# Adjacency blocks turned by DMA, one gathered tile looked up, twelve low parts by GpSimd

## What is computed

```python
# layer 0: 8 nearest neighbours by ctx, 4 blocks
idx = top_k(-d2, 8)
for i in range(4):
    p = leaky_relu(points, 0.01)
    g = group(p, idx)
    points = (w_center[i] @ p + sum_k(w_neighbor[i] @ g)) / 9 + points
# layer 1: 30 nearest neighbours by the same ctx
rel = pts[idx30] - pts                       # 3 coordinates
feat = [rho, theta, phi] and the same minus their mean
h = 3 small layers with batch norm and leaky_relu(0.2)
att = softmax(h)                             # over the 30 neighbours
out = x + sum_k(att * x[idx30])
```

## Time and profile before

| | us |
|---|---|
| median of 3 runs | 698.96 |
| lowest, highest | 698.92, 703.58 |
| the profiled execution, its own time | 703.56 |
| its span | 701.8 |
| TensorE busy | 679.3 (97%) |
| VectorE busy | 599.0 (85%) |
| ScalarE busy | 346.1 (49%) |
| GpSimd busy | 394.1 (56%) |

### The profile page before, as it was taken

How to read it: one execution, slowest core, us unless ns; L and a number is a source line. 1 busy time by engine, 2 the same in 40 slices (tenths; PEclk the granted TensorE clock), 3 DMA queues, 4 the chain that set the end, 5 groups by cost and what they waited for, 6 DMA issues and landing times.

```text
span 701.8 us, 13118 instructions
## 1 busy us (share of the span) xinstructions
PE 679.3 (97%) x5364; PEld 573.4 (82%) x5364; DVE 599.0 (85%) x879; ACT 346.1 (49%) x529; POOL 394.1 (56%) x324
## 2 busy tenths in 40 slices
PE   5999999999999999999999999999999999999998
PEld 4799889878888887788888987987988877778887
DVE  4699999999789899876679998776895999788866
ACT  6456547347525327766694354384473434233210
POOL 2268757664877877310039677558669865610143
PEclk9999999999999999999999999999999999999999
DMA  9630300200000022644532721713627763621125
GB/s 350 192 4 2 120 1 2 90 21 11 1 2 0 2 65 87 221 152 165 164 114 91 116 79 63 118 61 91 105 76 221 126 90 90 182 77 47 46 92 164
DMA packets 39483, 64.89 MB, mean 92 GB/s; under 512 B 16000, under 2 KB 16256, under 8 KB 39424
## 3 DMA queue, kind: packets, MB, share of 16 engines
q1 hardware_dynamic: 30288, 44.61, 18.9%
q0 software_dynamic: 8608, 18.40, 13.7%
q10 hardware_dynamic: 528, 1.05, 0.4%
HBM read 47.92 MB, written 14.82 MB: 89 GB/s over the span
## 4 chain that ended last, share of the span: by engine, by line
PE 60%; DVE 16%; POOL 11%; issue 5%; ACT 4%; DMA 2%; another core or an unknown queue 1%; SPq 0%; POOLq 0%; DVEq 0%; ACTq 0%
PE bank L1669 17%; PE bank L1731 4%; PE bank L1579 4%; PE bank L1693 4%; PE bank L1581 4%; PE bank L1580 4%; PE bank L1694 4%; PE bank L1695 4%; POOL more L660 4%; PE bank L1834 3%; PE bank L1793 3%; PE bank L1836 3%; PE bank L1835 3%; POOL p_second L590 3%; POOL pts_l L601 2%
## 5 line engine op out<-in xcount | busy, mean ns | idle before, releaser
L1669 PE MATMUL bank<-nbr,pts_h 128*128 128x512 f32 (+2 forms) x512 | 192.9, 379 | 3.2 <-POOL pts_l L601 1.6
L1669 PE MATMUL bank<-nbr,pts_l 128*128 128x512 f32 (+2 forms) x512 | 190.1, 374 | 0.0
L590 POOL TENSOR_TENSOR p_second<-p_first,p_second 128x512 f32<-128x512 f32 x58 | 76.4, 1320 | 99.4 <-ACT p_second L868 99.3
L1669 PEld LDWEIGHTS bank<-nbr,pts_h 128*128 128x128 f32 x512 | 96.6, 189 | 20.8 <-POOL pts_l L601 3.4
L1669 PEld LDWEIGHTS bank<-nbr,pts_l 128*128 128x128 f32 x512 | 96.7, 189 | 14.9 <-issue 0.2
L882 ACT CAST pts_h<-bank 128x512 fp32r<-128x512 f32 (+2 forms) x64 | 35.1, 554 | 144.5 <-PE bank L1669 136.0
L1693 PE MATMUL bank<-wT,pts_h 128*128 128x512 f32 x256 | 102.7, 401 | 1.4 <-DVE pts_l L1172 0.7
L1695 PE MATMUL bank<-wT,pts_l 128*128 128x512 f32 x256 | 100.4, 392 | 0.0
L1694 PE MATMUL bank<-wT,pts_h 128*128 128x512 f32 x256 | 100.2, 392 | 0.0
L601 POOL TENSOR_TENSOR pts_l<-p_second,pts_h 128x512 fp32r<-128x512 f32 x58 | 79.1, 1370 | 3.5 <-ACT pts_h L874 2.0
L1579 PE MATMUL bank<-pts_h 128*128 128x512 f32 (+3 forms) x192 | 68.9, 359 | 8.6 <-DVE pts_l L1098 8.1
(11 more groups left out here) (228 smaller groups left out, 1518.5 us busy)
## 6 DMA issues: line engine op xcount, KB each, us to landing
p_rows<-p_second SPq DMA_DIRECT2D x32, 256.0 KB, 2.0
more<-a_rows SPq DMA_DIRECT2D x16, 480.0 KB, 4.7
scratch<-a_rows SPq DMA_DIRECT2D x14, 480.0 KB, 5.0
X<-in_ctx SPq DMA_DIRECT2D x12, 512.0 KB, 6.1
out_dram<-X SPq DMA_DIRECT2D x15, 256.0 KB
more<-in_ctx SPq DMA_DIRECT2D x4, 512.0 KB, 5.7
X<-in_x SPq DMA_DIRECT2D x2, 1024.0 KB, 5.5
x_rows<-X SPq DMA_DIRECT2D x8, 256.0 KB
```

Source lines behind the costliest of these rows:

```text
L590: pool.tensor_tensor(p, a, b, ALU.subtract).then_inc(s_p32, 1)
L1669: mm = pe.matmul(bank[u % 3][:, 0:w], p[:, m, t * P:(t + 1) * P], nbr[b][:, m, hf * HALF:hf * HALF + w], start=(m == 0 and part_ == 0), st ...
```

## The change

- The blocks of the adjacency are turned by 16 DMA transposes on SP's queue instead of 128 TensorE transposes, and land in SBUF: row blocks 0 to 6 in the place of nbr0's last eighth, the others in scratch. SP takes turns 0 and 1 ahead of the loads of X for batch 0, turns 2 to 5 and 6 to 9 ahead of the two loads for batch 1, the rest behind them.
- Row block 0 is looked up like the others (32 lookups instead of 30); the table in DRAM, its three stores and the 30 gathers go.
- The low parts of q of units 10 to 15 (pass 1) and 16 to 21 (pass 2) are made by GpSimd; ScalarE copies the bank to one of three buffers in scratch for it, right behind the high part.
- Tables: VectorE's selection ends at step 39 instead of 43, with 4 steps in step 0 instead of 6, and 6 in step 16 instead of 2; adjacency in steps 4, 7, 10, 14 instead of 3, 6, 9, 14; `G0` 42 instead of 44, `M0` 60 instead of 61; network entries 0 to 10 a step earlier, then an empty step; ScalarE's arctan a step after VectorE's entry 10. `T0` is step 109 in both.

```diff
+        with nc.sbuf_tensor("nbr0_land", [P, NT, N], F32) as nbr0_land:
+            pass
         nbr0 = sb("nbr0", [P, NT, N], F32R)
...
+        def landing(T):
+            if T < NT - 1:
+                c0 = (NT - 1) * P + T % 2 * P // 2
+                return nbr0_land[:].bitcast(BF16)[:, :, 2 * c0:2 * c0 + P]
+            o = (SC + 1) * N + T % 2 * HALF
+            return scratch[:, o:o + HALF].bitcast(BF16).rearrange("p (m n) -> p m n", m=NT)
...
+        Q_POOL = [2 * CT + j for j in range(2, 8)] + [4 * CT + j for j in range(6)]
+        q32 = [scratch[:, 6 * N - (3 - i) * HALF:6 * N - (2 - i) * HALF] for i in range(3)]
+
+        def pooled(u):
+            return sum(q <= u for q in Q_POOL)
...
-            n = STEPS_AT[g % 16] + {0: 4, 1: 1}.get(g, 0)
+            n = STEPS_AT[g % 16] + {0: 2, 1: 1, 15: 1, 16: 4, 18: 1, 20: 1, 22: 1, 34: 1}.get(g, 0)
...
-        ADJ_AT = {3: (8, 9), 6: (10, 11), 9: (12, 13), 14: (14, 15)}
+        ADJ_AT = {4: (8, 9), 7: (10, 11), 10: (12, 13), 14: (14, 15)}
...
-        ROWS_AT = {30: 0, 33: 1, 36: 2, 44: 3}
+        ROWS_AT = {28: 0, 31: 1, 34: 2, 41: 3}
...
-        G0 = max(SEL_AT) + 1
-        M0 = G0 + LOOKUPS // 2 + 2
+        G0 = 16 * 2 + 10
+        M0 = G0 + TILES + 2
...
-               ((8, 1),), ((9, 0),), ((9, 1),), ((9, 2),), (10,), (11,), (12,), (13,), (14,), (15,), (16,), ((21, 0),),
+               ((8, 1),), ((9, 0),), ((9, 1),), ((9, 2),), (10,), (), (11,), (12,), (13,), (14,), (15,), (16,), ((21, 0),),
...
+            def adj_turn(T):
+                sp.wait_ge(s_diag, T + 1)
+                if T == NT - 1:
+                    sp.wait_ge(s_sqmm, 2 * NH)
+                if T >= 2:
+                    sp.wait_ge(s_nbr, T - 1)
+                sp.dma_start_transpose(landing(T), adj[:, T % 2, :]).then_inc(s_adjT[T % 2], 16)
+
+            adj_turn(0)
+            adj_turn(1)
             for i, (t0, t1) in enumerate(((0, 4), (4, 8))):
...
+                for T in (range(6, 10) if i else range(2, 6)):
+                    adj_turn(T)
...
+            for T in range(NT + 2, TILES):
+                adj_turn(T)
+            sp.wait_ge(s_nbr, TILES)
...
+            def q_low(g):
+                pool.wait_ge(s_q32, pooled(g))
+                pool.tensor_tensor(q_l[:, g % (2 * CT), :], q32[pooled(g) % 3], q_h[:, g % (2 * CT), :].bitcast(F32),
+                                   ALU.subtract).then_inc(s_qlp, 1)
...
-                    for i in range(done, done + GATHER_AT.get(g, 0)):
...
-                        pool.indirect_dma_start(
-                            out=near_rows[:, i // K1, i % K1, :], out_offset=None, in_=tab_d,
...
+                    if s_ < 2 * CT and 2 * CT * it + s_ in Q_POOL:
+                        q_low(2 * CT * it + s_)
...
             def nbr_out(T):
-                act.wait_ge(s_adjT, T + 1)
+                act.wait_ge(s_adjT[T % 2], 16 * (T // 2 + 1))
...
-                         bank[6 + T % 2][:].bitcast(BF16).rearrange("p (m n) -> p m n", m=NT)) \
-                    .then_inc(s_nbr, 1)
+                         landing(T)).then_inc(s_nbr, 1)
...
                 act.copy(q_h[:, j, 0:w], bank[g % 3][:, 0:w]).then_inc(s_qh, 1)
+                if g in Q_POOL:
+                    if pooled(g) == 1:
+
+                        act.wait_ge(s_nbr, TILES)
+                    elif pooled(g) > 3:
+                        act.wait_ge(s_qlp, pooled(g) - 3)
+                    act.copy(q32[pooled(g) % 3], bank[g % 3][:]).then_inc(s_q32, 1)
...
+                if 10 in NET_AT.get(g - 1, ()):
+                    act.wait_ge(s_mlp, MLP["atan"])
+                    act.activation(pair(6), tmp, ACT.Arctan).then_inc(s_act, 1)
...
-            def adj_turn(T):
-                pe.wait_ge(s_diag, T + 1)
-                if T >= 2:
-                    pe.wait_ge(s_nbr, T - 1)
-                for m in range(NT):
-                    mm = pe.transpose(bank[6 + T % 2][:].bitcast(BF16)[:, m * P:(m + 1) * P],
-                                      adj[:, T % 2, m * P:(m + 1) * P], ident_b[:])
-                mm.then_inc(s_adjT, 1)
...
+                    if u - 3 in Q_POOL:
+                        pe.wait_ge(s_q32, pooled(u - 3))
+                    elif u >= 3:
+                        pe.wait_ge(s_ql, u - 2 - pooled(u - 3))
```

More of the change, by code:

```diff
@@ L269, in build @@
         s_diag = sem("adj_diagonal_ready")
-        s_adjT = sem("adj_transposed")
+        s_adjT = [sem(f"adj_transposed{i}") for i in range(2)]
         s_nbr = sem("nbr_ready")
@@ L279, in build @@
         s_qh = sem("q_high_ready")
+        s_q32 = sem("q_copied")
+        s_qlp = sem("q_low_by_gpsimd")
         s_ql = sem("q_low_ready")
@@ L380, in build @@
         NET_AT = {M0 + i: items for i, items in enumerate(NET)}
-        T0 = M0 + len(NET) + GT
+        T0 = 16 * (ITS - 2) + 13
         S0 = T0 + 6
@@ L458, in store_p @@
                     else:
-                        sp.wait_ge(s_look, LOOKUPS)
+                        sp.wait_ge(s_look, 2 * TILES)
                     i, count = own_landed(it, e)
@@ L463, in _ @@
             for c in range(CHUNKS):
-                for t in range(2 * CH) if c else range(2 * GT, 2 * CH):
-                    u = 2 * CH * c + t - 2 * GT
+                for t in range(2 * CH):
+                    u = 2 * CH * c + t
                     if u == 0:
                         sp.wait_ge(s_arow, 16 * (CHUNKS - 1))
+                    if u == 2:
+                        sp.wait_ge(s_qlp, len(Q_POOL))
                     if u == 3:
@@ L655, in gather @@
                     else:
-                        pool.wait_ge(s_look, LOOKUPS)
+                        pool.wait_ge(s_look, 2 * TILES)
                 else:
@@ L793, in nbr_out @@
             def nbr_out(T):
-                act.wait_ge(s_adjT, T + 1)
+                act.wait_ge(s_adjT[T % 2], 16 * (T // 2 + 1))
+                if T == NT - 1:
+                    act.wait_ge(s_nbr, T)
                 if T == NT:
@@ L933, in side @@
                     a_row_out(TURN_AT[g])
-                if 0 <= g - G0 < LOOKUPS // 2:
+                if 0 <= g - G0 < TILES:
                     onehot_a(2 * (g - G0) + 1)
@@ L945, in side @@
                         act.activation(slots(6, 2), slots(4, 2), ACT.Sqrt).then_inc(s_act, 1)
-                    if m == 10:
-                        act.wait_ge(s_mlp, MLP["atan"])
-                        act.activation(pair(6), tmp, ACT.Arctan).then_inc(s_act, 1)
                     if m == 14:
@@ L1163, in q_low @@
                 j = g % (2 * CT)
+                if g in Q_POOL:
+                    return
                 dve.wait_ge(s_qh, g + 1)
@@ L1200, in pick_r @@
             def pick_r(u):
-                T, k0 = GT + u // 2, (u % 2) * KH
+                T, k0 = u // 2, (u % 2) * KH
                 dve.wait_ge(s_af, T // CH + 1)
@@ L1297, in network @@
                 if n == 0:
-                    dve.wait_ge(s_rows, 16 * GT * K1)
-                    link(dve.tensor_copy(near[:, :, 0:GT, :], near_rows[:].rearrange("p t k j -> p j t k")))
                     tt(grid(0), grid(0), own_k[:, 0], ALU.subtract)
@@ L1467, in side @@
                     index_rows(ROWS_AT[g])
-                if 0 <= g - G0 < LOOKUPS // 2:
+                if 0 <= g - G0 < TILES:
                     onehot_a(2 * (g - G0))
                 for u in (2 * (g - G0) - 4, 2 * (g - G0) - 3):
-                    if 0 <= u < LOOKUPS:
+                    if 0 <= u < 2 * TILES:
                         pick_r(u)
@@ L1647, in _, with low_ready @@
             gram(15)
-            adj_turn(6)
             norms(1)
+            def low_ready(u):
+                pe.wait_ge(s_ql, u + 1 - pooled(u))
+                if pooled(u):
+                    pe.wait_ge(s_qlp, pooled(u))
             def aggregate(g, units=1):
@@ L1727, in lookup @@
                 pe.wait_ge(s_ar, CHUNKS)
-                b = (GT + u // 2) // NT
+                b = u // (2 * NT)
                 for k in range(KH):
@@ L1742, in side @@
             def side(g):
-                if g == 1:
-                    adj_turn(NT - 1)
-                for T in ADJ_AT.get(g - 1, ()):
-                    adj_turn(T)
                 if g in TURN_AT:
```

34 lines of the change are left out of this document (4 added, 30 removed).

## The result

The changed kernel takes 696.33 us (median of 20 runs, 694.29 to 699.21); the kernel before, measured beside it, 699.7 us (20 runs). The ratio is 0.9945, 95% interval 0.993 to 0.996: 3.9 us faster, and within 1%. On a second chip the ratio was 0.9935 (0.9923 to 0.9948), with 694.9 us. The profiled span fell from 701.8 to 697.5 us.

What follows compares the result with a forecast made beforehand. TensorE was taken to bound the kernel, with VectorE nearly full too during the selection. The terms -2.2 + 2.4 + 1.3 - 4.2 - 1.0 = -3.7 us took the median 698.96 to 695.3 us, range 689.3 to 704.

Steps and rivals of the forecast that it cites:

- A DMA turn: Adjacency turns: 4 us from GpSimd's diagonal to the landing, 1.5 us between two; nothing lost up to about 4.5 us.
- Rival A: Late DMA turns: whole gain gone at 5.7 us a turn, 705.8 us at 8, 712 at 10.1; chance 0.20.
- the slope of 3 us per us: Each us of a turn beyond about 4.5 us is paid in all three critical adjacency pairs.
- Before pass 0: Seven TensorE turns stand before pass 0; removing them gains TensorE 3.5 to 4.0 us.
- the two waits of 2 and 1.8 us: Pass 0: TensorE, 4 us earlier, waits for VectorE's low parts at 136.8 and again at the next unit.
- the step that failed: Start of pass 1: GpSimd's last low parts of p still end at 190.98, cutting the gain to 2.3 us.
- rival C: All given back: VectorE's extra pass 1 steps miss its gap, products wait 1 to 4 us, near 698; chance 0.10.
- +2.4: Two more lookups for tile 0, where TensorE sets the pace, cost 2.4 us.
- +1.3: Pass 2 steps with lookups: ScalarE's list takes 5.35 us against TensorE's 5.1; five steps at 0.26 cost 1.3 us.
- The start of the lookups: Waits before the first lookups and the clock's dip after them go: -4.2 us, or -2.9 if the dip stays.
- The arctan: Network steps 0 to 10 earlier, ScalarE's arctan a step after VectorE's: TensorE's wait at 427.43 goes, -1.0 us.
- The sign that was named: No wait before ScalarE's arctan, where it waited 5.29 us for VectorE at 422.90.

Runs made afterwards that it cites:

- experiment 4: Changed kernel with each of turns 8 to 13 made twice, one after the other: 710.82 us, ratio 1.0158 to the kernel before.
- Experiment 5: Changed kernel with adjacency pairs (10,11) and (12,13) one step earlier, at steps 6 and 9: 696.06 us, ratio 0.9957 to the kernel before.
- experiment 6: Also written `tables_old`: changed kernel with the step tables of the kernel before, all other parts kept: 702.05 us, ratio 1.0015 to the kernel before.
- after_again: The changed kernel itself, measured again on the chip of the gather runs: 694.9 us, ratio 0.9935 to the kernel before.
- experiment 7: Also written `net_late`: changed kernel with ScalarE's arctan at its old place and network entry 10 a step later: 697.26 us, ratio 0.9944 to the kernel before.
- gather_low: Changed kernel with row block 0 gathered again, 30 gathers in steps 38, 39 and 48 to 53: 697.93 us, ratio 0.9984 to the kernel before.
- dve_low: Changed kernel with all low parts of q on VectorE again, without ScalarE's twelve copies: 698.83 us, ratio 0.9995 to the kernel before.
- turns_alone: The kernel before with only the turns by DMA; its own tables, gathers and low parts kept: 697.39 us, ratio 0.9952 to the kernel before.
- gather_np3: gather_low with units 0 and 1 of pass 3 one after the other, not paired: 696.96 us, ratio 0.9964 to the kernel before.
- gather48: gather_np3 with the 30 gathers in steps 48 to 55, none in 38 and 39: 721.98 us, ratio 1.0317 to the kernel before.

## Why the prediction was right, point by point

The time (696.33 for 695.3) and the ratio (0.9945, the sum's being 0.9947) were right. The mechanism was right in the main: two engines without slack let TensorE keep only a part of the 8.2 us. The terms were less so: a gain that was 1.2 us too small and a cost 0.8 too high stood against gains that were 1.2 and 0.6 us too large. That the sum fits to 0.2 us is luck.

**A DMA turn: right.** Taken as 4 us from diagonal to landing; 3.2 us from issue to landing. Rival A, late turns, is out, but its mechanism is real: experiment 4 gives 14.9 us for twice the turns, where the slope of 3 us per us was argued. The price by the Trainium skill, VectorE: DVE Perf Modes, section The three transpose paths (1309 ns for a 128 x 128 block, so the prediction's estimate of 10.5 us for eight in a row), does not hold here: all eight blocks in one DMA of 128 x 1024 landed in 3.2 us. The page gives a lone block; adding it up was the prediction's step. The copies 2 and 3 were said to be 3 us late; the wait was 2.50.

**Before pass 0: 2.7 us, not 3.5 to 4.0.** One of the seven turns stood in a wait that TensorE has anyway: where turn 6 was, at 127.3, it now waits 0.55 us for GpSimd, at 126.2. The rest of the difference, 0.3 us, is not traced.

**Pass 0: the two waits of 2 and 1.8 us did not come.** There is one, 1.48 us, as there was before. TensorE, 2.7 us ahead and not 4, comes to the unit at 138.1 (136.8 forecast), and the first low part is at 137.15 (138.3 forecast), so it is in time. Pass 1 starts at 180.1, not 181.

**Pass 1: the step that failed.** I held that GpSimd hardly gets earlier and that its last low part, at 191, cuts the gain to 2.3 us. It ended at 188.2, 2.8 us earlier; the prediction had named low parts that end well before 191 as a sign of being wrong:

```profile
161.93 2.56 POOL L612 TENSOR_TENSOR p_second<-p_first,p_second 128x512 f32<-128x512 f32 x2 [0.61 <-ACT p_second L889]
164.44 1.30 POOL L623 TENSOR_TENSOR pts_l<-p_second,pts_h 128x512 fp32r<-128x512 f32 x1
168.47 0.43 POOL L571 TENSOR_TENSOR scratch<-scratch,ident_b 128x128 bf16<-128x128 bf16 x1 [2.73 <-ACT scratch L827]
...
185.70 2.51 POOL L623 TENSOR_TENSOR pts_l<-p_second,pts_h 128x512 fp32r<-128x512 f32 x2
```

A join and a low part more (2.5 us) now run ahead of diagonal 12, in idle time in which GpSimd did one join before; the diagonal itself is at 168.5 for 168.7. Experiment 5 takes them away again, and the last low part ends 1.2 us later. I had written that diagonal 12 stands one join later and not drawn the conclusion: work ahead of a wait is a gain for a chain that runs back to back behind it. TensorE so came out of the pair 5.2 us ahead (its last eighth at 188.2 + 0.9 for 194.3), and what cut the gain from there to 3.4 us was VectorE. The added work of 4.6 us did not fit into its gap of 5.4 us without a wait, it filled it, and some 1.1 us of TensorE's time by starts goes in waits at 231. That is rival C in part. Forecast -2.2 at pass 2, measured -3.4.

**The lookups: +2.4 right; +1.3 too high.** ScalarE's list does set the pace of these steps, 5.19 us a step for 5.35 forecast; its one-hots stand back to back:

```profile
277.85 1.89 ACT L927 ACTIVATE more<-more,minus_part 128x1920 bf16<-128x1920 bf16 x1
...
283.03 1.89 ACT L927 ACTIVATE more<-more,minus_part 128x1920 bf16<-128x1920 bf16 x1
```

TensorE needs 5.11 for such a step where nothing holds it (294.87 to 299.98 in the kernel before), so five steps cost some 0.5 us.

**The start of the lookups: -4.2, of which -3.0 came.** The waits and the late products before them (2.9 us) are gone. So is the fall of the clock at the first lookups (1.3), but the one at 311 us is longer by 1.2 us (6.08 for 4.85) in the profiled execution. Over the executions on record, span times (1 - mean granted clock) is 2.7 us for the kernel before (92, beside the experiments) and 1.3 for the changed kernel (25), so in the mean 1.4 us of it is won. The cause was half right: by the traces of experiment 6 most of it goes with the moved low parts and the turns, and only a wait of 0.45 us with the tables.

**The arctan: -1.0 forecast, and not by its cause.** Pass 4 gained 0.4 us (48.5 for 48.9; 0.9 in `after_again`), and experiment 7 shows that the arctan's place has no part in it that can be seen. The sign that was named, no wait before ScalarE's arctan, did not come: it still waits 4.2 us (5.29 before), but TensorE no longer waits behind it. In experiment 6, where the network starts later, TensorE waits 2.4 us in pass 4 and its clock falls.

The sum with the measured terms is -3.4 + 2.4 + 0.5 - 3.0 - 0.4 = -3.9 us. The trace has -3.3 at the start of pass 5, so 0.6 us of it is not accounted for, and -4.3 at the end. (The last step, in pass 6, goes with a wait of 1.15 us for GpSimd at 486.9 that only the trace of before has.)

## What to carry over

Work taken off the engine that is full pays only up to the next engine without slack: look for it stage by stage, and for what stands behind a wait in each engine's list. An edit that fills another engine's gap, to the last us, is paid a little later. Measure a helper's gathers at the place where they are to stand: moving 6 of 30 gathers to other steps made the kernel 25 us slower here, and why stays open.

## What the hardware showed

- One DMA transpose of 128 x 1024 in bf16, SBUF to SBUF, landed in 3.2 us (median of nine; 3.4 of the other seven).
- TensorE's granted clock fell to half (1.2 GHz) for 3.4 us after waits of 1.9 us (`gather_low`), 2.0 us (`dve_low`, `turns_alone`) and 2.4 us (`tables_old`), and for 3.4 or 6.8 us at 180 matmuls of 24 columns in a row. After waits of 1.9 and 2.1 us in `gather_np3`, 2.0 us in `tables_old` (at 140.8) and 2.2 us in `net_late`, and after waits of 1.3 and 1.5 us in the changed kernel, it stayed full. With the 180 split by an aggregate it stayed full in most executions (13 of 20). The same kernel runs with and without the fall: the changed kernel's executions at 1.000 took 695.6 us in the mean (6), those at 0.995 699.1 (2).
- TensorE's streams of small matmuls have gaps that nothing in the profile explains: 3.1 us where the attention is spread after the change (3.2 before), 17.0 us in the lookups of `gather48`. From the last pass's first product to the end, where the program is the same in all these kernels, they take 136.8 us (`gather_low`, 0.5 us of such gaps) to 140.6 (`tables_old`, 2.6 us of gaps, and 1.7 us at half clock after the longest, 2.1 us). The changed kernel itself took 139.4 us there in its first trace and 136.8 in its second. TensorE's longest group of them in the changed kernel, of the waits of the whole kernel:

```profile
PE bank L1809 <- issue: 3.1, 5, 1.4
```
